# A three-block transformer kernel whose normalizations get their scale from another sequence of operations, and two of which become one pass

## The reference, cut to what matters

```
def _layernorm(x, axis=-1, eps=1e-05):
    m = jnp.mean(x, axis=axis, keepdims=True)
    v = jnp.var(x, axis=axis, keepdims=True)
    return (x - m) / jnp.sqrt(v + eps)
...
x = x + 0.5 * _L0_ffn_ref(_layernorm(x, axis=-1), ...)    # mixture of experts: moe0
x = x + _L0_attn_ref(_layernorm(x, axis=-1), ...)         # 16 heads: heads
x = x + 0.5 * _L0_ffn_ref(_layernorm(x, axis=-1), ...)    # moe1
x = x + 0.5 * _L1_ffn_ref(_layernorm(x, axis=-1), ...)    # recurrent: cell0
x = x + _L1_attn_ref(_layernorm(x, axis=-1), ...)         # decayed attention and MLP: decay
x = x + 0.5 * _L1_ffn_ref(_layernorm(x, axis=-1), ...)    # cell1
```

## Time and profile before

| | |
|---|---|
| median of 3 runs | 2816.11 us (2814.51 to 2816.17) |
| the profiled execution's own time | 2814.1 us |
| its span | 2812.3 us |
| PE busy in the span | 2633.2 us (94%) |
| DVE busy | 2253.9 us (80%) |
| ACT busy | 1829.7 us (65%) |
| POOL busy | 1232.4 us (44%) |

### The profile page before, as it was taken

The page is one execution under the profiler, slowest core; times in us unless marked ns, Lnnn a source line. Parts: engine busy times, 40 slices in busy tenths (PEclk is TensorE's granted clock), DMA queues, the critical chain, the costliest instruction groups (busy, mean ns, idle before and its releaser), DMA issues. The chain is left out here.

```text
span 2812.3 us, 36464 instructions
## 1 busy us (share of the span) xinstructions
PE 2633.2 (94%) x11619; PEld 1977.0 (70%) x11619; DVE 2253.9 (80%) x3349; ACT 1829.7 (65%) x3092; POOL 1232.4 (44%) x1265
## 2 busy tenths in 40 slices
PE   7899999997999999999999997999999989788788
PEld 4688888874666666666666664888888866577566
DVE  5777777777999999999999978777787765578545
ACT  3355555556888888888888863555555555466565
POOL 2466667664232323233333312666666650345200
PEclk9999999998999999999999999999999999789899
DMA  2566666644333333333333323466666610100000
GB/s 63 125 140 137 147 140 131 148 99 150 103 101 103 101 105 99 106 98 107 101 104 100 106 71 75 108 147 143 134 147 146 132 42 1 38 8 8 8 8 30
DMA packets 107391, 271.55 MB, mean 97 GB/s; under 512 B 30784, under 2 KB 35648, under 8 KB 107072
## 3 DMA queue, kind: packets, MB, share of 16 engines
q1 hardware_dynamic: 82192, 235.41, 33.8%
q0 software_dynamic: 24576, 33.62, 4.3%
q10 hardware_dynamic: 432, 0.20, 0.0%
HBM read 258.35 MB, written 10.76 MB: 96 GB/s over the span
## 5 line engine op out<-in xcount | busy, mean ns | idle before, releaser
L628 POOL TENSOR_TENSOR moe_experts_lo<-moe_experts_hidden,moe_experts_hi 128x512 fp32r<-128x512 f32 x512 | 660.9, 1291 | 342.2 <-ACT moe_experts_hi L566 342.1
L909 DVE TENSOR_TENSOR heads_e_lo<-heads_e,heads_e_hi 128x1024 fp32r<-128x1024 f32 x512 | 616.2, 1224 | 25.8
L573 ACT ACTIVATE psum<-psum 128x512 f32<-128x512 f32 x512 | 298.0, 582 | 479.4 <-PE psum L90 479.4
L743 POOL DMA_DIRECT2D heads_left<-heads_parts x512 | 306.7, 612 | 670.2 <-PE psum L797 610.6
L849 ACT ACTIVATE heads_e<-psum 128x1024 f32<-128x1024 f32 x512 | 520.0, 1023 | 107.2 <-PE psum L797 107.2
L600 DVE TENSOR_TENSOR moe_experts_weighted<-moe_spread,psum 128x512 f32<-128x512 f32 x512 | 351.1, 686 | 190.7 <-PE psum L90 186.8
L88 PE MATMUL psum<-heads_e_hi,heads_v_lo 128*128 128x512 f32 x1024 | 429.6, 419 | 18.1 <-DVE heads_u L875 18.1
L88 PE MATMUL psum<-moe_n_hi,moe_w_lo 128*128 128x512 f32 x1024 | 400.8, 391 | 6.0 <-PEq L54 6.0
L89 PE MATMUL psum<-heads_e_lo,heads_v_hi 128*128 128x512 f32 x1024 | 404.1, 395 | 0.0
L90 PE MATMUL psum<-heads_e_hi,heads_v_hi 128*128 128x512 f32 x1024 | 400.9, 392 | 0.0
L89 PE MATMUL psum<-moe_n_lo,moe_w_hi 128*128 128x512 f32 x1024 | 400.1, 391 | 0.0
(11 more groups left out here) (412 smaller groups left out, 4314.3 us busy)
## 6 DMA issues: line engine op xcount, KB each, us to landing
moe_spread<-moe_mask SPq DMA_DIRECT2D x128, 1024.0 KB, 10.4
heads_right<-heads_parts SPq DMA_DIRECT2D x512, 64.0 KB
heads_left<-heads_parts POOLq DMA_DIRECT2D x512, 64.0 KB, 2.5
heads_scale<-heads_inverse_copy SPq DMA_DIRECT2D x64, 512.0 KB, 3.7
moe_experts_raw<-in_gate SPq DMA_DIRECT2D x16, 256.0 KB, 11.7
moe_experts_raw<-in_up SPq DMA_DIRECT2D x16, 256.0 KB, 11.7
moe_experts_raw<-in_down SPq DMA_DIRECT2D x16, 256.0 KB, 11.7
heads_parts<-heads_e_hi SPq DMA_DIRECT2D x16, 256.0 KB, 2.4
```

The costliest lines, as they stand in the source:

```text
L573: act.activation(psum[:, GATE + p % 2, :], psum[:, GATE + p % 2, :], ACT.Silu).then_inc(silu_ready, 1)
L628: pool.tensor_tensor(lo[:, p, :], hidden[:, p % 2, :], f(hi[:, p, :]), ALU.subtract).then_inc(low_ready, 1)
L743: eng.dma_start(f(tile[row:row + 2 * HEAD, h % 2, :]), parts_dram[dims, order:order + 2, at]).then_inc(loaded[h % 2], 16)
L909: dve.tensor_tensor(e_lo[:, s, :], e[:, s % 4, :], f(e_hi[:, s, :]), ALU.subtract).then_inc(low, 1)
```

## The change

The variance becomes one full product for each chunk: a matrix of 1/128 as weights, the squares as the moving operand, so it arrives on all partitions, in PSUM. ACT takes its logarithm (with epsilon as bias) and then the exponential of -1/2 times that, which is the scale on all partitions. The copy of the centered chunk, the square root, the reciprocal, the diagonals and the spread product are gone; `scaled` reads the centered chunk from PSUM and the scale from SBUF. The rounding to fp32r goes from ACT to DVE, behind `scaled`. The table set with logarithm and exponential is loaded ahead of the first square. PSUM is four banks of centered chunks and four of variances.

The pass decay_norm is gone. decay_norm1 (now decay_norms) writes the once normalized residual and the twice normalized chunk from the same centered chunk: with v the variance, the second scale is (v (1 + eps) + eps^2)^(-1/2), which takes a second logarithm and a second exponential on ACT and a second multiplication on DVE.

```diff
-                    after(pe, deviation_ready, c - 1)
-                    for q in range(PARTS_OF_CHUNK):
-                        last = pe.matmul(psum[:, VARIANCE + c % 2, q:q + 1], squares[:, c % 3, q * P:(q + 1) * P],
-                                         inv[:, 0:1], start=q == 0, stop=q == PARTS_OF_CHUNK - 1, skip_group_check=True)
-                    last.then_inc(variance_ready, 1)
-
-                def spread(c):
-                    pe.wait_ge(diagonal_ready, c + 1)
-                    after(pe, scaled_ready, c - BANKS + 1)
-                    pe.matmul(psum[:, SCALE + c % BANKS, :], f(ones), diagonal[:, c % 2, :, :].rearrange("p a b -> p (a b)"),
-                              start=True, stop=True).then_inc(scale_ready, 1)
+                    after(pe, log_ready if keep is None else both_log_ready, c - BANKS + 1)
+                    pe.matmul(psum[:, VARIANCE + c % BANKS, :], inv, squares[:, c % 3, :], start=True,
+                              stop=True).then_inc(variance_ready, 1)
...
-                    after(act, scaled_ready, c - RING + 1)
-                    act.copy(centered[:, c % RING, :], psum[:, CENTERED + c % BANKS, :]).then_inc(centered_ready, 1)
...
+                    act.activation(logs[:, c % 2, :], psum[:, VARIANCE + c % BANKS, :], ACT.Ln, bias=eps).then_inc(log_ready, 1)
+                    if keep is not None:
+                        act.activation(both_logs[:, c % 2, :], psum[:, VARIANCE + c % BANKS, :], ACT.Ln,
+                                       scale=1.0 + EPS, bias=columns["eps_squared"]).then_inc(both_log_ready, 1)
+
+                def take_scales(c):
+                    after(act, scaled_ready, c - SCALES + 1)
+                    act.wait_ge(log_ready, c + 1)
+                    act.activation(scales[:, c % SCALES, :], logs[:, c % 2, :], ACT.Exp, scale=-0.5).then_inc(scale_ready, 1)
+                    if keep is not None:
+                        act.wait_ge(both_log_ready, c + 1)
+                        act.activation(both_scales[:, c % SCALES, :], both_logs[:, c % 2, :], ACT.Exp,
+                                       scale=-0.5).then_inc(both_scale_ready, 1)
+
+                act.preload_act_table_set("natural_log_exp_and_others")
+                for c in range(CHUNKS + 2):
                     if c < CHUNKS:
                         square(c)
+                    if c >= 2:
+                        take_scales(c - 2)
                     if 1 <= c <= CHUNKS:
-                        root(c - 1)
-                    if keep is None and c >= 4:
-                        high(c - 4)
+                        take_logs(c - 1)
...
                     dve.wait_ge(scale_ready, c + 1)
-                    dve.tensor_tensor(to, centered[:, c % RING, :], psum[:, SCALE + c % BANKS, :],
-                                      ALU.mult).then_inc(scaled_ready, 1)
+                    if keep is not None:
+                        dve.tensor_tensor(keep[:, chunk(c)], scale, psum[:, CENTERED + c % BANKS, :], ALU.mult).then_inc(kept_ready, 1)
+                        scale = both_scales[:, c % SCALES, :]
+                        dve.wait_ge(both_scale_ready, c + 1)
+                    dve.tensor_tensor(to, scale, psum[:, CENTERED + c % BANKS, :], ALU.mult).then_inc(scaled_ready, 1)
                     if affine is not None:
                         dve.wait_ge(scaled_ready, c + 1)
                         dve.tensor_scalar(to, to, affine[0], affine[1], ALU.mult, ALU.add).then_inc(normal_ready, 1)
 
-                for c in range(CHUNKS + 2):
+                def high(c):
+                    dve.wait_ge(normal_ready, c + 1)
+                    dve.tensor_copy(n_hi[:, chunk(c)], normal[:, c % RING, :]).then_inc(high_ready, 1)
+
+                for c in range(CHUNKS + 1):
                     if c < CHUNKS:
-                        diagonals(c)
-                    if 1 <= c <= CHUNKS:
-                        scaled(c - 1)
-                    if keep is None and c >= 2 and c - 2 in VECTOR_LOWS:
-                        take_low(dve, "vector", c - 2)
+                        scaled(c)
+                        high(c)
+                    if c - 1 in VECTOR_LOWS:
+                        take_low(dve, "vector", c - 1)
...
-        layernorm(nc, f"{tag}_norm", psum, consts, x, None, None, keep=residual)
...
-            layernorm(nc, f"{tag}_norm1", psum, consts, residual, n_hi[:, :], n_lo[:, :],
+            layernorm(nc, f"{tag}_norms", psum, consts, x, n_hi[:, :], n_lo[:, :], keep=residual,
                       affine=(columns["ln1_g"], columns["ln1_b"]), splits=splits,
```

More of the change, by code:

```diff
@@ L132, in layernorm @@
               splits=(), loads=(), copies=None, copied=None, x_dram=None):
-    center, inv, eps, identity, ones = (consts[name] for name in ("center", "inv", "eps", "identity", "ones"))
-    PARTS_OF_CHUNK = BANK // P
-    COLUMNS = TOKENS // P
-    CENTERED, VARIANCE, SCALE = 0, 3, 5
-    BANKS = 3
+    center, inv, eps, columns = (consts[name] for name in ("center", "inv", "eps", "columns"))
+    CENTERED, VARIANCE = 0, 4
+    BANKS = 4
     RING = 4
+    SCALES = 3
     VECTOR_LOWS = (2, 5, 7)
@@ L145, in layernorm @@
         squares = sb(f"{tag}_squares", [P, 3, BANK])
-        centered = sb(f"{tag}_centered", [P, RING, BANK])
-        deviation = sb(f"{tag}_deviation", [P, COLUMNS])
-        inverse = sb(f"{tag}_inverse", [P, COLUMNS])
-        diagonal = sb(f"{tag}_diagonal", [P, 2, PARTS_OF_CHUNK, P])
+        logs = sb(f"{tag}_logs", [P, 2, BANK])
+        scales = sb(f"{tag}_scales", [P, SCALES, BANK])
         normal = sb(f"{tag}_normal", [P, RING, BANK])
-        difference_ready, centered_ready, squares_ready, variance_ready = (
-            sem("difference"), sem("centered"), sem("squares"), sem("variance"))
-        deviation_ready, inverse_ready, diagonal_ready = sem("deviation"), sem("inverse"), sem("diagonal")
-        scale_ready, scaled_ready = sem("scale"), sem("scaled")
+        difference_ready, squares_ready, variance_ready = sem("difference"), sem("squares"), sem("variance")
+        log_ready, scale_ready, scaled_ready = sem("log"), sem("scale"), sem("scaled")
         normal_ready = scaled_ready if affine is None else sem("normal")
@@ L164, in chunk @@
             return slice(c * BANK, (c + 1) * BANK)
-        def columns(c):
-            return slice(c * PARTS_OF_CHUNK, (c + 1) * PARTS_OF_CHUNK)
         def take_low(eng, who, c):
@@ L200, in difference @@
                         pe.wait_ge(x_loaded[c], 16)
-                    after(pe, centered_ready, c - BANKS + 1)
+                    after(pe, scaled_ready, c - BANKS + 1)
                     pe.matmul(psum[:, CENTERED + c % BANKS, :], center, x[:, chunk(c)], start=True,
@@ L232, in square, with take_logs @@
                     act.activation(squares[:, c % 3, :], psum[:, CENTERED + c % BANKS, :], ACT.Square).then_inc(squares_ready, 1)
-                    after(act, scaled_ready, c - RING + 1)
-                    act.copy(centered[:, c % RING, :], psum[:, CENTERED + c % BANKS, :]).then_inc(centered_ready, 1)
-                def root(c):
+                def take_logs(c):
                     act.wait_ge(variance_ready, c + 1)
-                    act.activation(deviation[:, columns(c)], psum[:, VARIANCE + c % 2, 0:PARTS_OF_CHUNK], ACT.Sqrt,
-                                   bias=eps).then_inc(deviation_ready, 1)
@@ L241, in high @@
-                def high(c):
-                    act.wait_ge(normal_ready, c + 1)
-                    act.copy(n_hi[:, chunk(c)], normal[:, c % RING, :]).then_inc(high_ready, 1)
-                for c in range(CHUNKS + 4):
+                    act.activation(logs[:, c % 2, :], psum[:, VARIANCE + c % BANKS, :], ACT.Ln, bias=eps).then_inc(log_ready, 1)
+                    if keep is not None:
+                        act.activation(both_logs[:, c % 2, :], psum[:, VARIANCE + c % BANKS, :], ACT.Ln,
+                                       scale=1.0 + EPS, bias=columns["eps_squared"]).then_inc(both_log_ready, 1)
@@ L295, in _ @@
                     pool.tensor_tensor(lo, raw[:, :], f(hi), ALU.subtract).then_inc(split_low, 1)
-                if keep is None:
-                    for c in range(CHUNKS):
-                        if c not in VECTOR_LOWS:
-                            take_low(pool, "pool", c)
+                for c in range(CHUNKS):
+                    if c not in VECTOR_LOWS:
+                        take_low(pool, "pool", c)
 def route_and_share(nc, tag, psum, consts, router, weights, n_hi, n_lo, mask_dram, x, spread_body):
@@ L1647, in decayed_attention_layer @@
         mlp_layer(nc, f"{tag}_mlp", psum, consts, w, (h_hi, h_lo), residual, x)
[L1651 removed]
+VECTORS = ("gate_b", "p_b", "out_b", "clock_b", "one", "tiny", "eps_squared", "ln1_g", "ln1_b", "ln2_g", "ln2_b", "b2",
            "b1_0", "b1_1", "b1_2", "b1_3", "bf", "bi", "bc", "bo", "in_c")
@@ L1704 @@
         "tiny": np.full(P, 1e-8, np.float32),
```

(1 more changed line is left out.)

32 lines of the change are left out of this document (11 added, 21 removed).

## The result

The kernel after the change takes 2740.88 us (median of 4 runs, 2737.46 to 2743.51); the kernel before took 2815.31 on the same chip (4 runs, 2813.82 to 2816.17). The ratio is 0.9746, with a 95% interval from 0.9722 to 0.9770: some 71 us less. The two medians by themselves are 74.4 us apart, which lies inside that interval. The forecast was 2755 with a range from 2738 to 2774, so the time lies inside the range, near its lower end and 14 us under the likeliest value.

What follows compares the result with a forecast made beforehand. PE was taken to set the pace of the normalization passes, 2.61 us per chunk. Seven passes saving 56.4 us plus 3 for the clock level gave 59.4 off 2814.1, so 2755 us, range 2738 to 2774.

Steps and rivals of the forecast that it cites:

- The pace of PE: Ordinary pass at full clock: two full products in a row, 1.80 us per chunk instead of 2.61.
- ACT: Ordinary pass: square, logarithm and exponential take 1.65 us per chunk, under PE's 1.80; one table load per pass.
- The rival of two loads per chunk: Logarithm and exponential each load a table, 2 x 1.28 us per chunk on ACT: 2855 to 2870 us; chance 0.03.
- The merged pass: Decay's two passes become one of 29.3 us, DVE 2.85 and ACT 2.75 per chunk; saves 23.4 us.
- The ring of four banks: PSUM banks held from difference to `scaled`: a chain of some 5.5 us against 7.2, so it should not close.
- DVE as the bound of all passes (2780): Each rounding takes 1.28 us beside POOL, DVE 2.3 per chunk, 25 us more together: 2780; chance 0.12.
- the mark set in the prediction (0.9): Sign of being wrong: the mean time of the rounding on DVE is over 0.9 us.
- Heads: Heads pass: SP's 24 copies, spaced about 0.58 us, end it; 28.0 us against 33.4, saves 5.4.
- moe1: moe1's pass: `scaled` of chunks 4 to 7 waits a little for POOL's work; 21.2 us against 25.7, saves 4.5.
- The lower clock level: PE's 1.2 GHz stretch in moe0, decay_norm2 and cell1 ends earlier: between 0 and 17 us, taken as 3.
- early-clock rival: PE's lower clock level ends early everywhere: 2740 us; chance 0.09.
- The rival on the other side: PE stays at the lower level through all passes, 3.70 us per chunk: 5 us slower, 2819; chance 0.04.

Runs made afterwards that it cites:

- rounding_on_act: The changed kernel with the rounding moved from DVE back to ACT, three chunks behind: 2742.74 us, ratio 0.9770 to before; again 2748.03 us, 0.9767.
- the experiment with pieces: The changed kernel with the head weight's split on POOL in four pieces of 512 columns: 2739.97 us, ratio 0.9742 to the kernel before.
- More low parts on DVE: The changed kernel with the head weight split in four and five of eight low parts on DVE in heads and moe: 2737.21 us, ratio 0.9734.
- The wide versions: The kernel before with variance products of 64 or 128 columns instead of 1: 2798.43 us (64), 2800.39 and 2798.56 us (128).

## Why the prediction was right, and where it was off

**The pace of PE.** Two full products per chunk: forecast 1.80 us, measured 1.71. The 0.94 of the earlier trace rows was the step from a spread product behind single columns; between two products of one kind it is 0.86. cell0, where no other thing interferes, came out at 21.2 against 21.3: the shorter pace is 0.7 us over eight chunks, and its last rounding, which stands in the drain, took 0.78 instead of 0.42.

**ACT.** Forecast 1.65 us per chunk, the logarithm 0.69 and the exponential 0.63. Measured 0.68 and 0.62 (means of L223 and L231, 679 and 624 ns). Three instructions take 2.09 - 0.51 = 1.58 us by the four of the rounding_on_act timeline. One table load per pass at its start, as forecast (L237 x7); that of the merged pass starts at 2343.56 and the first square at 2344.86, so it lies under the first products. The rival of two loads per chunk is out.

**The merged pass.** Forecast 29.3 with DVE the bound at 2.85 per chunk and ACT next at 2.75; measured 27.9 with ACT the bound at 2.65. The forecast named the wrong one of two near neighbours. DVE was busy for 2.53: gain and offset took 0.61 instead of 0.69, and the instruction behind a rounding of 0.43 starts 0.09 before its end, an overlap that the forecast had counted for the first `scaled` only. The ring of four banks closed here, which I had said should not happen. With a round of 2.65 set by ACT that is the form that ACT's pace takes on PE, not a bound of its own: ACT has no gap between its first logarithm and its last exponential.

**DVE as the bound of all passes (2780).** It did not come. The mean of the rounding is 0.43 and 0.44 in decay and 0.58 in the cell stage. It is 0.84 in moe and 1.18 in heads, and by the mark set in the prediction (0.9) the heads value was over it, through one instance of 4.26 us. The argument against the rival held in its result and not in its reason. I had written that the next rounding mostly finds POOL idle. Outside decay it did so for 12 of 40, which took under 0.5 us; 24 took 0.54 to 1.00, and four took 1.47 to 4.26 beside splits of weights. The mean of all 56 is 0.70, near the 0.62 of the sum and far from the rival's 1.28, and the excess mostly fits under PE's pace. The Trainium skill's rule that the prediction cites (GPSIMD Engine Reference, "Specifications", with VectorE: DVE Perf Modes, "Mode 2×_2P"), by which such a copy within SBUF contends with GpSimd for a shared interface, is borne out by this trace: a cast of 0.43 alone is 1.00 beside a low part of POOL and 4.26 beside the large split.

**Heads.** Forecast 28.0 with SP's last copy near 654, which is 26.7 into the pass; measured 27.9, with the last copy 26.3 into it (644.33 - 618.00). The spacing of 0.58 and the 24 copies were the term that carried this, and the experiment with pieces confirms it.

**moe1.** Forecast 21.2, measured 22.3. The likely cause is the rounding's 0.84 and POOL's 16.1 us of splits and low parts, which I had let cost "a little"; with the rounding on ACT and the same high start the pass was 21.6. More low parts on DVE took 0.6 of it back. The share of each isn't separated.

**The lower clock level.** This is the term that was mis-sized: 3 us beside 17.3 in three passes, where 12.4 beside 17.3 was measured. Not all of the 12.4 is the clock: in decay_norm2 DVE sets the round, and it was 2.07 us between roundings where the forecast had 2.2, some 0.9 over seven rounds. I had bounded the term by 0 and 17 and taken a value near the lower end, with the early clock as a rival of 0.09 chance at 2740 us. The step that failed is "I take a small part of it": the old kernel had full products in every chunk too, and was low for 15 us all the same, so the single columns were the suspicious thing, and I gave their removal too little. The wide versions show that their width alone is worth 10 to 14 us by the times. What the traces also showed is that the earlier trace rows caught an execution in which three passes were long where another had two (moe1 and heads). The long passes of the profile were not a fixed property of moe0, decay_norm2 and cell1, and a forecast made from one trace carries this.

The mechanism of the early-clock rival is what happened. That the time meets its 2740 to the microsecond is luck: the level gave at most 12.4 of its 17 us, and the rest came from the merged pass, from the stages between the passes and from a profiled execution above its median. The range held, but its upper bound is not what its words say: half of the way to the rival at 2780 is 2767, not 2774.

**The rival on the other side** (PE low in all passes, 2819) had no part: the merged pass leaves PE idle for about a third of each chunk, and its products remain at 1.02 to 1.13 us.

**The sum.** 10 of the 14 us by which the time lies under the forecast are in the passes. Of the rest, 1.6 stands in the stages between them, and 2.6 in the profiled execution being above the median of its runs (2743.51 against 2740.88).

## What to carry to other kernels

A statistic that every partition needs can be worth computing at full width: here one product with a constant matrix and two table functions from one set cost 0.86 us of PE and 1.3 us of ACT per 512 columns, and did away with a chain across three engines. The same plan with a reciprocal over 512 columns on DVE was 178 us slower than this, and 107 slower than the kernel before.

Two normalizations in a row can share their centered input; that gave 14.8 of the 24.8 us here, and it moves the bound from PE to the engine that makes the scales.

A stretch at the lower clock level has to be looked at in more than one trace before it is given to a pass. Where single-column products stand between full ones, widening them is worth a try even if the extra columns are thrown away; here 64 or 128 columns gave 10 to 14 us, and 32 gave nothing that the times can tell.

## What the runs showed of the hardware that I had not expected

- Small products of 128 columns instead of 1 cost PE no time at the full clock: eight of them take 1.05 us instead of 0.95, the full products around them take 1.02 instead of up to 1.10, and the round is 2.61 us in both.
- With products of 1 and of 32 columns between the full ones, PE stayed at 1.2 GHz for 13 to 16 us in 6 of 13 passes that began at that level, though it had no gap there; in the versions with 64 and 128 it did so in none of 12.
- Reciprocal on DVE: 3.35 us for 128x512, against 0.69 for a multiplication and 0.43 for a cast of that shape.
- A normalization pass that PE begins at the lower level is 1.4 to 1.5 us longer than the same pass begun at the higher (cell0 23.1 and 21.7 with the rounding on ACT, the merged pass 29.4 and 27.9). Which it is changes between executions.
- An ACT instruction in a row without gaps gets longer in the records while the pace stays. The logarithm of the merged pass goes from 0.69 at 2346.67 to 0.83 at 2364.79, with starts 2.65 to 2.67 apart until the seventh chunk; in cell0, where ACT pauses, it stays at 0.67 to 0.69. The distance between starts is what to sum there, not the duration.
- The stage between decay's passes and decay_norm2, which no edit touches, took 203.4 to 212.4 us in different executions. This is as much as several of the effects above, and the reason why single times could not tell them.
